# First causal stage: where the causal mask of units 0 and 2 of each pair is added to the scores

## The reference, cut to what matters

```python
qkv = x @ w_qkv                      # x: rows normalised first (pre-norm)
q, k, v = split(qkv)                 # 16 heads, head width 16
scores = einsum('bhqd,bhkd->bhqk', q, k) / sqrt(16)
scores = where(tril, scores, -1e9)   # causal mask
a = softmax(scores, axis=-1)
o = einsum('bhqk,bhkd->bhqd', a, v)
x = x + o @ w_proj
```

## Time and profile before

| | us |
|---|---|
| median of three runs | 3740.81 (3737.97 to 3741.61) |
| the profiled execution | 3764.06 |
| its span, first to last instruction | 3762.2 |
| of it, the first causal stage, from the first score to the last add | some 310 (24 to 334) |

### The profile page before, as it was taken

The page is one execution under the profiler, slowest core; times in us unless marked ns, Lnnn a source line. Parts: engine busy times, 40 slices in busy tenths (PEclk is TensorE's granted clock), DMA queues, the critical chain, the costliest instruction groups (busy, mean ns, idle before and its releaser), DMA issues. The chain is left out here.

```text
span 3762.2 us, 71866 instructions
## 1 busy us (share of the span) xinstructions
PE 3498.5 (93%) x25820; PEld 2378.0 (63%) x25821; DVE 1912.7 (51%) x6167; ACT 1649.9 (44%) x3571; POOL 1560.2 (41%) x2142
## 2 busy tenths in 40 slices
PE   8997899997999678999799999999999989999997
PEld 5664555555666464444466666666666658899986
DVE  4664666664788555664455555554555447211113
ACT  4663455554777306777344444444444431111111
POOL 1001333333677424553355555555555547000025
PEclk9999999999999789999999999999999989999998
DMA  9401211110000253000100000000000001799962
GB/s 282 169 0 26 51 38 32 31 25 12 10 18 22 57 156 74 19 18 10 41 7 7 7 8 13 7 7 7 13 7 7 1 6 55 268 325 326 326 221 80
DMA packets 111420, 262.52 MB, mean 70 GB/s; under 512 B 24003, under 2 KB 70241, under 8 KB 95841
## 3 DMA queue, kind: packets, MB, share of 16 engines
q1 hardware_dynamic: 90208, 224.70, 18.6%
q0 software_dynamic: 16384, 26.29, 2.5%
q10 hardware_dynamic: 4608, 8.39, 0.6%
HBM read 196.61 MB, written 62.65 MB: 69 GB/s over the span
## 5 line engine op out<-in xcount | busy, mean ns | idle before, releaser
L2397 POOL TENSOR_SCALAR wide_probs<-wide_probs,wide_inverse 100x361 f32<-100x361 f32 x512 | 607.3, 1198 | 0.1
L2592 ACT ACTIVATE wide_probs<-wide_probs,wide_least 100x361 f32<-100x361 f32 x512 | 301.0, 589 | 615.6 <-DVE wide_least L2665 615.6
L2665 DVE CUSTOM_DVE_ANT_0 wide_probs<-banks,wide_bias 100x361 f32<-100x361 f32 x512 | 251.7, 529 | 217.3 <-issue 217.3
L2395 POOL TENSOR_TENSOR wide_hold_pool<-eps 100x1 f32<-100x1 f32 x256 | 51.1, 200 | 567.4 <-DVE wide_inverse L2671 567.3
L2453 PE MATMUL banks<-w_wide_v,wide_c 64*120 64x512 f32 (+1 forms) x1152 | 263.5, 589 | 2.5 <-DVE wide_v L2651 1.7
L2077 ACT ACTIVATE rot_h<-banks,w_rot_b 128x800 f32<-128x800 f32 x256 | 223.6, 924 | 88.5 <-PE banks L1951 85.3
L2447 PE MATMUL banks<-wide_c,w_wide_k 64*128 64x361 f32 x1536 | 255.9, 464 | 3.1 <-DVE wide_kT L2648 2.3
L2489 PEld LDWEIGHTS banks<-ident,wide_probs 100*120 100x120 f32 (+1 forms) x1536 | 157.3, 171 | 150.4 <-issue 118.3
L2475 PE MATMUL banks<-wide_kT,wide_qT 64*100 64x361 f32 x1024 | 220.4, 507 | 7.5 <-issue 7.5
L3096 ACT ACTIVATE tiles_hT<-banks 128x512 f32<-128x512 f32 x114 | 68.1, 597 | 346.3 <-PE banks L3012 346.3
L2671 DVE RECIPROCAL wide_inverse<-wide_rowsum 100x2 f32<-100x2 f32 x256 | 42.5, 166 | 341.7 <-ACT wide_probs L2592 341.7
(11 more groups left out here) (464 smaller groups left out, 7590.3 us busy)
## 6 DMA issues: line engine op xcount, KB each, us to landing
tiles_w<-in_moe_w SPq DMA_DIRECT2D x114, 1024.0 KB, 5.1
slots<-zeros SPq DMA_DIRECT2D x58, 512.0 KB, 5.6
cross_c<-in_ctxT SPq DMA_DIRECT2D x32, 270.8 KB, 4.3
wide_c<-in_ctxT SPq DMA_DIRECT2D x32, 270.8 KB, 4.2
mix_kT<-slots SPq DMA_DIRECT2D x32, 256.0 KB, 4.2
slots<-mix_kT ACTq DMA_DIRECT2D x32, 256.0 KB, 3.9
tiles_rows<-slots SPq DMA_DIRECT2D x57, 128.0 KB, 4.7
slots<-tiles_out SPq DMA_DIRECT2D x57, 128.0 KB, 4.9
```

Source lines behind the costliest of these rows:

```text
L2397: last = nc.gpsimd.tensor_scalar(t.probs[:, i % RING, j, :], t.probs[:, i % RING, j, :], t.inverse[:, i % RING, j:j + 1], None, ALU.mult)
L2592: last = nc.scalar.activation(t.probs[:, i % RING, j, :], t.probs[:, i % RING, j, :], ACT.Exp, bias=t.least[:, i % RING, j:j + 1], scale=-1.0,
L2665: last = nc.vector.tensor_tensor_reduce(t.probs[:, i % RING, j, :], scores(j), t.bias[:, :], -1.0, LARGEST, ALU.add, ALU.min, t.least[:, i ...
```

## The change

Units 0 and 2 of the first causal stage get no mask matmuls: their score matmuls open the PSUM group themselves. VectorE instead has three passes over these units: it adds the mask while it moves the scores from PSUM to `probs`, takes the maximum from `probs`, and subtracts it in `probs` in place. A new semaphore `masked` is raised behind the first pass, and `score` of units 1 and 3 waits for that one, no longer for `shifted`. Units 1 and 3 and the third stage stay as they were.

```diff
+        units_masked_later = () if mixture else (0, 2)
...
                 else:
-                    pe.wait_ge(a[i - 1].shifted, of.n)
+                    pe.wait_ge(a[i - 1].masked if i - 1 in units_masked_later else a[i - 1].shifted, of.n)
+                if i not in units_masked_later:
+                    for j in range(2):
+                        nc.tensor.matmul(scores(j), g.ident_b[0:S, 0:S], g.causal[:, :], start=True, stop=False)
                 for j in range(2):
-                    nc.tensor.matmul(scores(j), g.ident_b[0:S, 0:S], g.causal[:, :], start=True, stop=False)
-                for j in range(2):
-                    last = nc.tensor.matmul(scores(j), t.qT[tile_rows(j), of.buf, c, lane, :], t.kT[tile_rows(j), of.buf, c, :, lane, :], start=False, stop=True)
+                    last = nc.tensor.matmul(scores(j), t.qT[tile_rows(j), of.buf, c, lane, :], t.kT[tile_rows(j), of.buf, c, :, lane, :], start=i in units_masked_later, stop=True)
                 last.then_inc(a[i].scores_ready, 1)
...
+            def mask_and_shift(of, i):
+                dve.wait_ge(a[i].scores_ready, of.n)
+                rowmax, unit = t.rowmax[:, i % PROBS_RING, :, :], t.probs[:, i % PROBS_RING, :, :].rearrange("s (j h) k -> s j h k", j=2)
+                nc.vector.tensor_tensor(t.probs[:, i % PROBS_RING, :, :].rearrange("s (j h) k -> s j (h k)", j=2), g.psum[0:S, 0:2, 0:BLOCKS * S],
+                                        g.causal[:, :].unsqueeze(1).broadcast_to([S, 2, BLOCKS * S]), ALU.add).then_inc(a[i].masked, 1)
+                dve.wait_ge(a[i].masked, of.n)
+                nc.vector.reduce_max(rowmax, unit, AX.X).then_inc(a[i].rowmax, 1)
+                dve.wait_ge(a[i].rowmax, of.n)
+                nc.vector.tensor_tensor(unit, unit, rowmax.unsqueeze(3).broadcast_to([S, 2, BLOCKS, S]), ALU.subtract).then_inc(a[i].shifted, 1)
...
                 if here:
-                    shift(here, 0)
+                    mask_and_shift(here, 0)
...
                 if here:
-                    shift(here, 2)
+                    mask_and_shift(here, 2)
```

More of the change, by code:

```diff
@@ L140, in causal_phase @@
         s = semaphores(nc, ctx, name, "ones picked k_bias y yT_ready yT q_ready q k_ready k v_ready v rowsum heads headsT_ready headsT proj_ready added parts_zero")
-        a = [semaphores(nc, ctx, f"{name}{i}", "scores_ready rowmax shifted probs turned_ready probsT heads_ready parts_ready parts") for i in range(SCORE_UNITS)]
+        a = [semaphores(nc, ctx, f"{name}{i}", "scores_ready masked rowmax shifted probs turned_ready probsT heads_ready parts_ready parts") for i in range(SCORE_UNITS)]
         t = buffers(nc, ctx, name, y=[S, TURNS, LANES, D], yT=[P, DC, LANES, S], qT=[P, TURNS, DC, LANES, S], kT=[P, TURNS, DC, BLOCKS, LANES, S], v=[S, TURNS, LANES, NH, HD + 1],
```

## The result

| | before | after |
|---|---|---|
| median | 3739.42 us (3732.74 to 3744.19, 12 runs) | 3749.34 us (3747.21 to 3751.98, 12 runs) |
| ratio, 95% interval | | 1.0027 [1.0019, 1.0035] |
| period of a pair | 18.88 us | 19.37 us |

The period is the time from score 0 of the second pair to score 0 of the last, over 14, in the profiled execution.

What follows compares the result with a forecast made beforehand. TensorE's own work was taken to bound the stage, other engines close behind. 14 periods at +0.45 us (+6.3), first pair -0.9, last pair +0.3 gave +5.7: 3740.8 to 3746.5 us, range 3738 to 3755.

Steps and rivals of the forecast that it cites:

- The saving of 0.34: TensorE, per unit: without mask matmuls scores start 0.34 us earlier, the 0.09 us pause before 64-row matmuls staying.
- The three passes: VectorE, units 0 and 2: mask addition, maximum and subtraction take 3.01 us instead of 2.01, 1.00 more per unit.
- The second ring: Second half, unit 2 through VectorE and ScalarE's copies to make_v: TensorE waits 0.76 us; period 19.33, 0.45 more.
- The first ring's length: First half, unit 0's scores through VectorE and exponential to its transposes: 177.45 to 182.44, TensorE waiting 0.70 us.
- What the saving is worth in full: Per pair, were TensorE still the bound: 2 x 0.34 + 0.33 = 1.01 us shorter.
- A: First causal stage: TensorE stays the bound, 15 us less, 3726 us; chance 0.09.
- B: VectorE: passes out of SBUF are shorter, 0.06 us on each of two, giving 3743.7 us; chance 0.08.
- C: VectorE: SBUF passes stretched by GpSimd or traffic, 0.2 us each, +11 us, giving 3758 us; chance 0.11.
- Who ends TensorE's first wait: First half: TensorE idles 0.70 us before unit 0's transposes, released by ScalarE's exponential (L709 or L711).
- The maximum out of SBUF: VectorE's second pass, on 800 columns: between 0.95 and 0.99 us, taken as 0.97.
- Slack at make_v: Second half, kernel before: make_v starts at 192.93, right where TensorE arrives anyway, with no room left.
- The first pair, -0.9: First pair: the wait for DMA hides unit 0's effect and unit 2's masks come off, -0.9 us (-0.6 to -1.1).

Runs made afterwards that it cites:

- Unit 2 alone: The change for unit 2 of each pair only, unit 0 keeping its mask matmuls and two passes, against the kernel before: 3744.43 us, ratio 1.0013.
- the heads' copy between the copies of k: Changed kernel, with ScalarE's copy of the turned heads moved between the second and third copies of k; against the kernel before: 3734.73 us, ratio 0.9988.
- both orders: TensorE's and ScalarE's lists reordered in both halves of a pair, against the kernel before: with the change 3723.47 us, ratio 0.9963; without it 3736.83, 0.9998.
- late hand-back: Changed kernel, but scores 1 and 3 wait for the subtraction (`shifted`) as before the change; against the kernel before: 3759.84 us, ratio 1.0058.
- Unused semaphores: Kernel before, with the semaphores `masked` allocated in both stages but never used; against the kernel before: 3738.55 us, ratio 1.0002.
- four units: Changed kernel with TensorE's and ScalarE's lists reordered, and units 1 and 3 also masked by VectorE; against the kernel before: 3720.73 us, ratio 0.9962.

## Why the prediction was right in its direction, and 4 us short

The time lies 2.8 us above the predicted 3746.5 and within its range; the difference lies 4.2 above the forecast +5.7, since the median of before came out at 3739.4 and not at the 3740.8 on which the forecast stood. Against the kernel before the loss is 0.27%, just past the 0.2% that parts slower from same; to that side the prediction had given 0.29, to the other 0.61.

Right, by its own steps:
- **The saving of 0.34.** Score 0 starts 1.03 behind the first matmul of the projection (161.25 to 162.28); forecast were 177.45 - 176.41 = 1.04. The pause ahead of 64-row matmuls stays when the masks go. The rule that a change of tiling mode drains TensorE, from the Trainium skill (TensorEngine Tiling (Array Packing), Key Properties), agrees with that. Without the pause the 1.03 would have been 0.95.
- **The three passes.** 3.01 forecast, 3.04 measured (163.25 to 165.30 + 0.99 = 166.29).
- **The second ring.** Make_v was to start 15.93 behind score 0 (193.38 - 177.45) and starts 15.96 behind it (178.24 - 162.28), released by the heads' copy; the wait is 0.71 for a forecast 0.76. Unit 2 alone shows that this ring carries the loss, and the heads' copy between the copies of k takes it away.
- **The first ring's length.** The transposes start 4.97 behind score 0 (167.25 - 162.28), forecast 4.99.
- **What the saving is worth in full.** 1.01 us a pair if TensorE were the bound; 1.01 between the two kernels with both orders.
- **Rivals.** A falls: TensorE isn't the bound. B falls: the maximum out of SBUF takes 0.986, out of PSUM 0.981 in the median (0.956 to 0.992), and the subtraction takes 0.992 from either. By the prediction's estimate from the errata table of the Trainium skill (VectorE: DVE Perf Modes) SBUF passes would be 0.06 us shorter; on 800 f32 columns no run here shows it. C falls: the three lines spread over 2 ns.

Wrong or missing:
- **Who ends TensorE's first wait.** The prediction named the exponential alone (L711). The trace shows 0.59 ahead of turn_parts 2, released by `divide` of the pair before, which VectorE does behind the three passes (L886, L888: 166.21 to 166.91). The exponential ends at 167.19 and the transposes start at 167.25, so a second wait would have stood there if the first had not: two rings end within 0.1 us of each other. The forecast wait of 0.70 came out near the mark because they do; that is luck. I had looked at what is queued behind the third pass on ScalarE, and not at what is queued behind it on VectorE itself.
- **The maximum out of SBUF** was sized at 0.97 from 400 and 512 columns, and takes 0.986. With 0.99 for all passes the bounds gave a period 0.49 longer, which is what was measured. Over 14 periods that is 6.8 in place of 6.3, 0.5 us of the miss.
- **Slack at make_v.** "There is no room left" was nearly right: the kernel before was already 0.1 late there, and paid 0.07 more for weights not loaded ahead. It changed nothing for this forecast, but is what the orders take back, 0.14 a pair, even without the change.
- **The first pair, -0.9.** At equal clock the profiles say -0.8 (0.72) and -0.5 (1.00). But the first profile of before and that of the changed kernel differ by +0.55 (14.19 against 13.64), since the clock came back later in one. The term had the right sign and about the right size, and no place in a sum that is held against single executions.
- **The profiled execution.** 3769.8 was forecast for it, and 3748.59 measured: the profile of the kernel before was itself 27 us long. Behind the cross-attention it took 2854.8 us, the second profile of the same kernel 2828.0, the changed kernel 2830.1. The forecast for the median did not use this.
- **What is left.** With 6.8 from the periods, less some 0.8 at the start, plus the 0.3 forecast for the last pair, the rows account for 6.3 of the 9.9; the interval's near end is 7.1. So at least 0.8 us, and 3.6 by the medians, stay unexplained. The late hand-back misses in the same direction (15.6 against 16.4 at the near end), and in its profile one pair with a lower clock costs 1.6. The +0.3 can't be read: from the last score 0 to the end of the stage it takes 24.42 and 23.61 us in two profiles of the kernel before and 23.89 in the changed one. Unused semaphores don't show the rest. Where it lies in a profile can be read: the span of the changed kernel is 10.7 us longer than that of the second profile of before (3746.8 against 3736.1), 6.5 of them up to the last add of the first stage, and 4.2 in the stages behind, which the diff doesn't touch. From VectorE's first to its last instruction the cross-attention takes 571.2 and 571.7 us in two profiles of before and 573.8 in that of after, with mean granted clocks of 0.950, 0.951 and 0.944, and 571.5 to 575.5 among the experiments. The longest, both orders, has the lowest clock, 0.939. Before's second profile was taken to see whether it could show 574 too, and it didn't. But there is no pattern by edit: without any change to the masks the stage takes 574.5 under both orders and 571.5 with the unused semaphores, with the change 571.6 when the heads' copy is moved. Whether a first stage that ends later makes the clock behind it worse, or this is chance, no run settles. I leave it open.

## What to carry to other kernels

Before work is taken off the bounding engine and given to a half-idle one, write down, for each point where the bounding engine next needs that other engine's result, how much earlier than needed it arrives (the slack); the list behind the new instruction on its own engine counts as much as the list of the engine that it feeds. If the slack there and the saving together are smaller than the added latency, the change costs time, and its price is the added latency less both. The same change can still be right if work that is ready is put between: here moves on two lists, TensorE's and ScalarE's, turned +9.9 us into -13.8. When it works, look again before doing more of it: at four units the next ring had closed.

## What the runs showed of the hardware that I had not expected

The first pair's length is a matter of when TensorE's granted clock returns to its upper level. After a wait for the same DMA, the mean granted clock between 34 and 46 us lay anywhere between 0.72 and 1.00 of full speed, and the time to the second pair was 14.8 (0.72), 13.6 (0.86) or 12.1 us (1.00) for the same code. The length of the wait for the rows doesn't decide it. On VectorE it was 2.39 us in the profile of the unused semaphores, at 1.00, and 4.65 to 5.25 in those of the same first pair at 0.72 and 0.86; but with the late hand-back it was 4.60 at 1.00, and with both orders 1.76 at 0.86. A step of 2.7 us from the clock is as large as the differences that single profiles were to tell apart here.
